# A fused graph layer on one core: a per-row product of the layer norm moved from VectorE to GpSimd, and the eighth expert's weights handled later, behind the first row scatters

## What is computed

```
xn  = layernorm(x)
gnn = conv(relu(conv(xn)))               # conv(x) = x @ W0 + b0 + (mean of the neighbours' rows) @ W1 + b1
mix = linear attention over all nodes (8 heads), xn @ Wq, Wk, Wv, Wfc
x   = x + gnn + mix
xn2 = layernorm(x)
gate = top 2 of 8 experts by xn2 @ Wg + bg + bias, softmax over the two
x   = x + sum over the two experts e of gate_e * (relu(xn2 @ W1[e] + b1[e]) @ W2[e] + b2[e])
```

## Time and profile before

| | us |
|---|---|
| median of 3 runs | 2243.13 (2240.91 to 2246.61) |
| the profiled execution, whole | 2241.64 |
| its span, first to last instruction | 2240.1 |
| PE busy in the span | 2075.8 (93%) |
| DVE / ACT / POOL busy | 1551.8 (69%) / 1198.9 (54%) / 369.5 (16%) |

### The profile page before, as it was taken

How to read it: one execution, slowest core, us unless ns; L and a number is a source line. 1 busy time by engine, 2 the same in 40 slices (tenths; PEclk the granted TensorE clock), 3 DMA queues, 4 the chain that set the end, 5 groups by cost and what they waited for, 6 DMA issues and landing times.

```text
span 2240.1 us, 52353 instructions
## 1 busy us (share of the span) xinstructions
PE 2075.8 (93%) x15356; PEld 1310.5 (59%) x15357; DVE 1551.8 (69%) x4887; ACT 1198.9 (54%) x2466; POOL 369.5 (16%) x438
## 2 busy tenths in 40 slices
PE   3887888999999999999999988999999995999997
PEld 2676675555565555555454544444444443899996
DVE  6898987999999999999645544455555444455554
ACT  3677663555555555555656543444444443566664
POOL 2000000000000000000111111111111222466665
PEclk9999998999999999999999999999999997999998
DMA  3333227222222222222534336555555554565552
GB/s 94 90 89 96 81 96 210 116 116 113 111 114 116 116 116 114 110 111 116 179 132 166 111 115 227 194 194 200 199 201 198 192 194 162 138 97 92 90 92 43
DMA packets 158735, 299.12 MB, mean 134 GB/s; under 512 B 31774, under 2 KB 107855, under 8 KB 156419
## 3 DMA queue, kind: packets, MB, share of 16 engines
q1 hardware_dynamic: 131075, 243.66, 31.3%
q0 software_dynamic: 25856, 47.15, 9.3%
q10 hardware_dynamic: 1664, 6.35, 0.8%
HBM read 148.32 MB, written 144.19 MB: 131 GB/s over the span
## 4 chain that ended last, share of the span: by engine, by line
PE 68%; issue 13%; DVE 8%; DVEq 4%; DMA 2%; POOLq 2%; POOL 1%; ACT 1%; ACTq 0%; SPq 0%
PE bank L2272 44%; PE bank L2263 6%; PE bank L2513 6%; PE bank L2498 6%; DVEq L1166 2%; POOLq L843 1%; DVE big L1123 1%; DVE big L1136 1%; PE bank L2480 1%; DVEq L1132 1%; DVE big L1118 1%; PE bank L2280 1%; DVE big L1134 1%; DMA big<-rows_dram 1%; PE bank L2141 1%
## 5 line engine op out<-in xcount | busy, mean ns | idle before, releaser
L2272 PE MATMUL bank<-RW,big 128*128 128x512 f16 x4753 | 1149.1, 380 | 0.0
L2272 PEld LDWEIGHTS bank<-RW,big 128*128 128x128 f16 x4753 | 431.6, 98 | 385.0 <-issue 3.6
L1920 ACT ACTIVATE big<-bank 128x512 f16<-128x512 f32 (+1 forms) x640 | 364.2, 573 | 316.5 <-PE bank L2263 316.4
L1294 DVE TENSOR_TENSOR big<-iotaB,keys 128x512 f16<-128x512 f16 x1300 | 451.9, 417 | 7.9 <-issue 6.8
L2263 PEld LDWEIGHTS bank<-big 128*128 128x128 f16 x2560 | 190.9, 98 | 106.2 <-issue 1.4
L2263 PE MATMUL bank<-big 128*128 128x128 f16 x2560 | 247.5, 219 | 0.4 <-issue 0.4
L977 POOL DMA_INDIRECT out_dram<-big x112 | 179.9, 1606 | 110.1 <-ACT big L2066 74.7
L910 POOL DMA_DIRECT2D big<-in_L_ffn_W_dram x8 | 6.2, 778 | 1052.5 <-DVE R L1353 1051.7
L2057 ACT ACTIVATE big<-bank,b1A,iscA 128x256 f32<-128x256 f32 x224 | 114.2, 560 | 98.2 <-PE bank L2498 93.6
L2513 PE MATMUL bank<-RW,big 128*128 (+1 forms) x1344 | 157.7, 274 | 0.4 <-DVE big L1717 0.3
L2498 PE MATMUL bank<-big,RW 128*128 128x256 f16 x1344 | 156.3, 273 | 0.4 <-ACT big L2046 0.4
(11 more groups left out here) (421 smaller groups left out, 2925.4 us busy)
## 6 DMA issues: line engine op xcount, KB each, us to landing
big<-a_dram SPq DMA_DIRECT2D x48, 800.0 KB, 6.0
big<-a_dram SPq DMA_DIRECT2D x48, 768.0 KB, 4.3
a_dram<-big SPq DMA_DIRECT2D x49, 640.0 KB, 2.9
a_dram<-big SPq DMA_DIRECT2D x49, 512.0 KB, 2.6
a_dram<-big SPq DMA_DIRECT2D x49, 416.0 KB, 2.4
big<-rows_dram SPq DMA_DIRECT2D x56, 265.0 KB
big<-in_x_dram SPq DMA_DIRECT2D x96, 128.0 KB, 2.1
own_dram<-big SPq DMA_DIRECT2D x48, 256.0 KB, 2.5
```

Source lines behind the costliest of these rows:

```text
L1294: last = v.tensor_tensor(out[q].rearrange("p b (m k) -> p b m k", k=2), inturn(iotaB[:, :], QB, P // 2), twice(kd[:, q * QB:(q + 1) * QB, ...
L1920: a.activation(Ab[q][:, 0:n], banks[BB(q)][:, 0:n], ACT.Copy).then_inc(s_ab, 1)
L2272: last = mm(bank[:, :], blk(q, c), R2[:, u * 2 * D:(u + 1) * 2 * D], start=(i == 0), stop=(i == T - 1))
```

## The change

1. **Filing.** DVE's `inverse` keeps the reciprocal alone; the drain and the product `offs` go. GpSimd makes the product, 49 times, in a loop of its own behind its constants, each time behind a new semaphore `s_rstd`; `s_stat`, for which ACT waits, is now raised by GpSimd.
2. **PE after the hidden layer.** The wait for `s_yl` ahead of `tile0` goes; `tile0` waits block by block for the tiles of the last group. The small product for the gate's bias (L2454) moves from ahead of `tile0` to behind it, and DVE's copy of it (L1665) moves down a few lines.
3. **The eighth expert.** On ACT `norms(7)` and `highs(7, 0)` move from behind `copy` of tile 0 to behind that of tile 1, and `highs(7, 1)` to behind that of tile 2. On DVE `scales(7)` moves from behind `finish2(0)` to behind `finish2(1)`, `lows(7)` to behind `finish2(2)`. On POOL `expert` is split in `drawn` (loads and reduction) and `kept` (store); `kept(7)` now stands behind `scatter(0)`, and the loads of RW for experts 0 and 1 behind `scatter(1)` and `scatter(2)`.
4. **SP.** The load of `b2b` and its wait for the eighth store move from ahead of `load_a(3)` to ahead of `load_a(48)`.

```diff
-            expert(0, True)
-            with pool.Fori(1, EXPERTS) as e:
-                expert(e, False)
+            drawn(0, True)
+            kept(0, True)
+            with pool.Fori(1, EXPERTS - 1) as e:
+                drawn(e)
+                kept(e)
+            drawn(EXPERTS - 1)
...
-            pool.wait_ge(s_yp, W + T)
-            pool.wait_ge(s_ap[1], 1)
-            for e in range(2):
-                weights(e)
...
+            for t in range(T):
+                i = t % 2
+                pool.wait_ge(s_rstd, t + 1)
+                nc.gpsimd.tensor_tensor(offs[:, i:i + 1], sums[:, i, 1:2], rstd[:, i:i + 1], ALU.mult).then_inc(s_stat, 1)
...
-                v.reciprocal(rstd[:, i:i + 1], sums[:, i, 3:4])
-                dve.drain()
-                v.tensor_tensor(offs[:, i:i + 1], sums[:, i, 1:2], rstd[:, i:i + 1], ALU.mult).then_inc(s_stat, 1)
+                v.reciprocal(rstd[:, i:i + 1], sums[:, i, 3:4]).then_inc(s_rstd, 1)
...
             iterate2(0, None, None)
+            iterate2(1, (0, 0), None)
             scales(EXPERTS - 1)
+            iterate2(2, (1, 1), (0, 0))
             for j in range(2):
                 lows(EXPERTS - 1, j)
-            iterate2(1, (0, 0), None)
-            iterate2(2, (1, 1), (0, 0))
...
-                    if i == 0:
-                        pe.wait_ge(s_yl, 1 + T)
                     u = 0 if i == T - 1 else T - 1 if i == 0 else i
+                    if i == 1 or u >= T - W:
+                        pe.wait_ge(s_yl, 2 + max(u, T - W - 1))
...
                 tile0(banks[5])
+                pe.wait_ge(s_gv, 1)
+                pe.wait_ge(s_ha, 8 * (T // W) + 4)
+                mm(banks[0][:, 0:8], ones[0:1, :], grows[0:1, 2, :], start=True, stop=True).then_inc(s_gp, 1)
```

More of the change, by code:

```diff
@@ L433, in gps_layer @@
         s_stat = sem("s_stat")
+        s_rstd = sem("s_rstd")
         s_std = sem("s_std")
@@ L725, in _ @@
             rows_x(1)
-            sp.wait_ge(s_wst, 16 * EXPERTS)
-            sp.dma_start(b2b.rearrange("p e n -> p (e n)"),
-                         io["L0_ffn_b2"].rearrange("(a e) n -> a (e n)", a=1).to_broadcast([P, EXPERTS * D]))\
-              .then_inc(s_b2, 16)
             load_a(3, 1, 2)
@@ L736, in _ @@
                     rows_x(t)
+            sp.wait_ge(s_wst, 16 * EXPERTS)
+            sp.dma_start(b2b.rearrange("p e n -> p (e n)"),
+                         io["L0_ffn_b2"].rearrange("(a e) n -> a (e n)", a=1).to_broadcast([P, EXPERTS * D]))\
+              .then_inc(s_b2, 16)
             load_a(T - 1, 0, T - 2)
@@ L903, in _, with drawn @@
                 pool.wait_ge(s_st[i], 16 * T + 16)
-            def expert(e, first):
+            def drawn(e, first=False):
                 if first:
@@ L918, in expert, with kept @@
                 nc.gpsimd.partition_all_reduce(nr3, sq3, P, RADD).then_inc(s_wr, 1)
+            def kept(e, first=False):
                 wait(s_wh, 2 * e + 2)
@@ L952, in scatter @@
                         in_=xrow[par].bitcast(F32)[0:rows, :], in_offset=None).then_inc(s_sx[par], 16)
-            with pool.Fori(0, T // 2 - 1) as k:
+            scatter(0, 0)
+            kept(EXPERTS - 1)
+            scatter(1, 1)
+            pool.wait_ge(s_yp, W + T)
+            pool.wait_ge(s_ap[1], 1)
+            weights(0)
+            scatter(2, 0)
+            weights(1)
+            scatter(3, 1)
+            with pool.Fori(2, T // 2 - 1) as k:
                 scatter(2 * k, 0)
@@ L1661, in _ @@
             v.tensor_copy(gpart[:, :, 2, :], gres2[:, :, :]).then_inc(s_gs, 1)
-            dve.wait_ge(s_gp, 1)
-            v.tensor_copy(gb, banks[0][:, 0:8]).then_inc(s_gv, 1)
             dve.wait_ge(s_yp, W + T)
@@ L1670, in _ @@
                 overflow(1, rd2)
+            dve.wait_ge(s_gp, 1)
+            v.tensor_copy(gb, banks[0][:, 0:8])
             v.memset(seen, 0.0)
@@ L1960, in aggregate @@
                 iterate(L, 0, None, banks[5])
-                if L == 1:
-                    norms(EXPERTS - 1)
-                    for j in range(2):
-                        highs(EXPERTS - 1, j)
                 if L == 0:
@@ L1970, in aggregate @@
                     iterate(1, 1, (0, 0, None), banks[7])
+                    norms(EXPERTS - 1)
+                    highs(EXPERTS - 1, 0)
                     iterate(1, 2, (1, 1, None), banks[5])
+                    highs(EXPERTS - 1, 1)
                     with act.Fori(1, T // 2) as k:
@@ L2386, in tiles2 @@
                 tile0(banks[5])
+                pe.wait_ge(s_gv, 1)
+                pe.wait_ge(s_ha, 8 * (T // W) + 4)
+                mm(banks[0][:, 0:8], ones[0:1, :], grows[0:1, 2, :], start=True, stop=True).then_inc(s_gp, 1)
                 pe.wait_ge(s_zc, 3 + T)
                 pe.wait_ge(s_gs, 1)
-                pe.wait_ge(s_gv, 2)
                 tile2(1, 1, 0, (0, 0), None, banks[7])
@@ L2449, in _ @@
             hidden(T // W - 1, 0, 16 * (T // W // 2 + 1))
-            pe.wait_ge(s_gv, 1)
-            pe.wait_ge(s_ha, 8 * (T // W) + 4)
-            mm(banks[0][:, 0:8], ones[0:1, :], grows[0:1, 2, :], start=True, stop=True).then_inc(s_gp, 1)
             with pe.If(lacking > 0):
@@ L2457, in _ @@
                 pe.wait_ge(s_zc, 3 + T)
-                pe.wait_ge(s_gv, 2)
+                pe.wait_ge(s_ha, 8 * (T // W) + 4)
                 overflow(1)
-            pe.wait_ge(s_yl, T)
-            pe.wait_ge(s_zc, T + 1)
+            pe.wait_ge(s_zc, 3 + T - W + max(i for i in range(W) if Y4(i) == 5) + 1)
             tiles2()
```

## The result

The changed kernel takes 2231.17 us (median of 5 runs, 2228.17 to 2233.39) against 2243.13 for the kernel before, measured beside it; the ratio is 0.9937, with a 95% interval of 0.9926 to 0.9948. That is 12 us less, where 22 were forecast: the time lies at the upper edge of the forecast's range (2214 to 2231), 10 us above its likeliest value. The span of the profiled execution fell from 2240.1 to 2229.3 us.

What follows compares the result with a forecast made beforehand. DVE bounds the filing, PE the second aggregation. Gains of 9.9 us in the filing and 12.1 behind the hidden layer sum to 22.0: 2221 us, range 2214 to 2231, whose upper end takes 7.4 instead of 12.1 upon rival A or C.

Steps and rivals of the forecast that it cites:

- Filing: DVE's one-hot follows the reciprocal sooner: 0.23 us a tile over 45 tiles, less 0.42 paid once; 9.9 us gained.
- The longer way of `offs`: Filing, DVE to POOL to ACT: L1820 starts 0.85 us after the reciprocal instead of 0.43; 0.42 paid once, at tile 45.
- Rival A: Filing: the port lock keeps DVE's next one-hot out 0.10 us a tile, 4.5 us in all; 2225.6 us, chance 0.13.
- C: Filing: one-hot waits until the reciprocal has left the pipe, gain 3.2 us, not 9.9; 2227.7 us, chance 0.07.
- D: Filing: POOL comes first in the lock and holds DVE 0.62 us a tile; 2249 us, slower, chance 0.04.
- PE behind the hidden layer: Start of second aggregation: no bias stall, then 3.3, 0.8 and 0.1 us at the transposes; gain 12.1 us with the clock.
- One eight at the lower clock: Second aggregation: eight blocks behind the 3.3 us stall take 3.62 us instead of 1.89, a loss of 1.7 us.
- The scatters: Second aggregation: tile 0's scatter, issued 9.5 us after tile 1's end, lands at 12 to 16.7, in time; stall 0.
- rival B: GpSimd's queue: `kept(7)` ahead of `scatter(1)` delays it; price 3 to 6 us, 2224 to 2227 us, chance 0.12.
- The prediction's own sign of being wrong: Second aggregation: the prediction is wrong if a new scatter wait appears at ACT's `high2(3)`; no size given.
- library switch: Inside rival B: POOL switches on either side of the 1 MB store; with it, might hold POOL 5 to 8 us longer.
- The load of `b2b`: SP, second aggregation: the moved 1 MB load of some 5 us ends before the next load of A; cost 0.

Runs made afterwards that it cites:

- e8: Changed kernel plus a useless 128x128 GpSimd sum ahead of each layer-norm product in the filing; 2235.33 us, 0.9948 of the kernel before.
- e10: Changed kernel with the filing's layer-norm product made on ACT instead of GpSimd; 2232.31 us, 0.9938 of the kernel before.
- e4: e3 with the eighth expert's store moved behind the scatter of tile 1; 2222.26 us, 0.9901 of the kernel before.
- e3: Changed kernel plus an always-met wait and one small GpSimd operation right behind the eighth reduction; 2224.41 us, 0.9910 of the kernel before.
- e7: Kernel before with part 2 alone (`tile0` right behind the hidden layer, bias product behind it); 2246.00 us, 1.0000 of the kernel before.
- e6: e4 with ACT's squares of the eighth expert behind its copy of tile 0; 2219.86 us, 0.9873 of the kernel before.
- e11: e6 with the eighth expert's two low halves parted, behind `finish2` of tiles 2 and 3, store behind scatter 2; 2217.94 us, 0.9879 of before.
- e2: Changed kernel with part 1 undone, product and drain back on DVE; 2241.45 us, 0.9984 of the kernel before.
- e5: Changed kernel with only the eighth expert's store moved behind the scatter of tile 1; 2232.69 us, 0.9936 of the kernel before.
- e9: Changed kernel with the eighth store issued behind scatter 3, its waits left behind scatter 0; 2225.43 us, 0.9909 of the kernel before.
- e12: The changed kernel measured again, nothing altered; 2233.41 us, 0.9945 of the kernel before.
- e1: Kernel before with part 1 alone, GpSimd making the filing's product; 2236.27 us, 0.9964 of the kernel before.

## Why the prediction was half right

**Filing, right.** Forecast 9.9 us. At ACT's L1820 of tile 45 it was 10.9, at the first aggregation 10.4. From tile 10 to 45 a tile became 9.03 / 35 = 0.26 us shorter, where 0.23 was taken; the step from the reciprocal to the one-hot went from 0.31 to 0.07. The longer way of `offs` was forecast at 0.85 and was 0.81. Rival A did not come (L1139 stands 0.75 behind L1134), and by e8 even a much longer GpSimd operation would cost 0.06 a tile, under the 0.10 of that rival; rivals C and D are far from these rows. e10 says the same from the other side: with the product on ACT a plain tile takes the same 4.53 us.

By the rule cited from the Trainium skill ("SBUF — State Buffer", section "SBUF: two separate sides"), whoever is second on the shared port pair blocks fully; it says so, among others, for a VectorE operation with two SBUF inputs against a GpSimd operation that reads SBUF. The trace agrees for the product, 0.54 us beside a one-hot. Beside DVE's 80x364 operations with one input of a decode tile it took 0.28. For DVE as the second, e8 shows a delay of 0.02 to 0.03 us and not a full block: DVE's second one-hot started at 288.40, while GpSimd's sum ran until 288.57.

**PE behind the hidden layer, right.** Stalls 0, 3.36, 0.63, 0 against 0, 3.3, 0.8, 0.1. One eight at the lower clock was forecast at 1.7 us and took 3.27 - 1.89 = 1.4; e4 had the same stall of 3.44 and full clock behind it, so this term is there in some executions only, and taking it at one eight was a choice that most profiles bear out.

**The scatters, wrong.** The forecast's likeliest case said that no scatter is late. Scatter 0 was not, as its step said (issued 9.7 us after the end of tile 1, at 1334.6; forecast 9.5). Scatter 1 was: issued at 25.7 us instead of the "about 20" that rival B gave, landed at 35.5 instead of 22.5 to 27, and PE stood at the transposes at 29.9 (forecast 29.8). It is rival B, with its place and its mechanism, given a chance of 0.12 and a price of 3 to 6 us. It cost 9.0: 3.2 for the late issue, 3.3 more with the store ahead in the queue, 2.4 for the lower clock; with the issue in time (e3) all three are gone.

The step that failed is the chain of POOL's queue from scatter 0 to scatter 1, in which the idle stretch ahead of the store's waits was put at nothing; it measured 11.63 us, 6.8 of them behind the low halves. The sign of it can be read off: the POOL row at 1367.46, used there only for its duration, has 9.99 us of idle ahead of it with nothing to name as its cause. That price was in a row I quoted. The prediction's own sign of being wrong, a new wait for a scatter at `high2(3)`, is the 9.08 us of ACT above; and the clock of this stretch is 0.92 where it wanted over 0.95. I counted the "library switch" as something that might take 5 to 8 us more than nothing, instead of putting these 9.99 us into the chain from scatter 0 to scatter 1 as a term: 1346.8 + 10 is already behind the slots of tile 1 (1354.6). The rest is the landing. The two issues start 1.4 us apart, for which the sum had no term, and the last one took 8.4 us from its start to landing, where the earlier trace rows give 2.4 to 7.2 for scatters that have no 1 MB store straight ahead of them.

The load of `b2b` in part 4 showed nowhere, but no run moves it alone. 22 - 9 = 13 us is what the forecast's own terms give with B at its measured price, against 12.0 and 13.3 measured.

That the time still lies at the edge of the range is luck. The upper end of 2231 was made of a worse second aggregation on top of rival A or C, and neither came; rival B, which did, was priced to end at 2227. By the prediction's own numbers the ends are also a little off: C with 4.7 us more is 2232.4, and 25.0 us of gain less 3 us of spread is 2215.

## What to carry to other kernels

When work is moved behind something on a queue, put every idle stretch of that queue into the sum, and above all one that the profile attributes to nothing: here 7 to 12 us of it stood ahead of the first ordinary GpSimd operation behind the last reduction over partitions, and it can be spent early by placing a small operation where GpSimd is idle anyway (one line, 7 to 9 us here), if that is early enough for what comes next (e6 and e11 were not). A stall that is removed only pays if the chain behind it has room; e7 shows one worth 4.1 us that paid nothing alone. A small elementwise operation that is taken off a saturated VectorE pays its issue and drain, 0.24 us here, as long as its consumer has that much slack, and a GpSimd operation beside VectorE's two-input ones ends when they end.

## What was not expected of the hardware

- The idle time ahead of the first ordinary GpSimd operation behind a reduction was 6.9 us (e3, e4), 9.8 (e6, e11) and 11.3 to 11.8 (e2, e5, e9 and the changed kernel). That it is a change of GpSimd's code fits its places; no run shows it. The page of the profile has a queue of kind "instruction", but with the same 99 packets and 1.62 MB in all fourteen profiles, and in the stretch of the changed kernel one packet of 16 KB, in e3's one of 8 KB, in those of e6 and e11 none. Nor does the load on the DMA engines explain its length: they were 25% busy in e3's (6.92 us), 53% in e4's (6.91), 91% and then 1% in e11's (9.75), and idle in the 7.14 us of before. Why the kernel before paid it once more on the way into the loop stays open.
- From the start of its last issue scatter 1 took 8.4 us to land in the changed kernel, with the 1 MB store issued 1.0 us ahead of the scatter; 6.1 in e9 without the store; 2.8 in e3 with the store issued 3.0 us ahead; the median of all scatters of before is 2.5. Scatter 0 took 6.1 in e6 with no store ahead.
- The clock behind a stall of PE: after 3.3 to 3.6 us ahead of the first transposes it was 1.2 GHz for most of the next eight blocks in the changed kernel, e2, e3, e5, e8, e9, e10 and e12 (3.0 to 3.5 us for the eight, 1.89 at full clock), and 2.4 in e4. After the 3.23 us ahead of e9's fourth it was 2.4. Behind the stall of before's third transposes (2.93 us) it was 2.4, in e7 (2.89) the eight took 2.71, in e1 (3.89) 3.44. After 0.3 to 1.5 us it was 2.4 in every profile, after 6.5 us or more 1.2 for most or all of the eight (3.2 to 3.6 us).
- GpSimd can be delayed by DVE for a whole instruction, while the one run that asks for the reverse (e8) has DVE delayed by 0.02 to 0.06 us.
